# Keys and values of a graph layer set anew: five norm batches, ScalarE shares the row norm, edge preparation moved forward

## The chip, the cores and the metric

One NeuronCore of a Trainium2 chip runs the whole program. The metric is the device time of one execution in microseconds (us); lower is better. The engines are TensorE (PE in the rows), VectorE (DVE), ScalarE (ACT), GpSimd (POOL) and SyncE (SP), which issues most DMAs.

## The reference, cut to what matters

A graph transformer layer on 3125 nodes of 256 channels and 50,000 edges, all in float32:

```
xn   = layernorm(x)
gate = sigmoid(silu(edge @ W1 + b1) @ W2 + b2)          # per edge
aggr = segment_sum(gate * xn[src], dst)
gnn  = xn + silu(concat(xn, aggr) @ U1 + c1) @ U2 + c2
q, k, v = xn @ wq.T, xn @ wk.T, xn @ wv.T               # 4 heads of 64
k, v = layernorm(k), layernorm(v)                       # per head
mix  = (q @ (k.T @ v / S)) @ wo.T + bo                  # per head, no softmax
x    = x + gnn + mix
x    = x + moe(layernorm(x))                            # 16 experts, top 2
```

The change lies in what comes before the edges: `xn`, the keys and values, their norms, and the sum `k.T @ v` over all nodes.

## The kernel before, in words

The 3125 rows lie in 25 tiles of 128 (`NT`). There is no scheduler: each engine runs its own list, written out by hand, and semaphores tie the lists together. The program has four long stretches: the keys and values (to about 100 us of the span), the edges in 98 groups of 512, the node update, and the experts. Only the first is touched.

In it a tile goes this way. VectorE takes mean and variance (`stats`, L1053, and `moments`, L1057). `layer_stats` makes 1/sqrt(variance) for a batch of tiles at once by twelve tiny instructions, each of which waits for the one before (L1048, L1037, L1038, and three rounds of L1040 to L1042); I call them links. Before, there are three batches: tiles 0 to 3, 4 to 9 and 10 to 24. `make_xn` (L1064) then writes the normalised row into one of four buffers; SyncE stores it to DRAM for the gathers of the edges. TensorE transposes it (L1618), ScalarE copies the transpose out (`copy_xt`, L752), and TensorE multiplies it by `wkv` (`project`, L1625, which holds both key and value weights). The head means are taken out of `wkv` itself, once: VectorE sums the heads (L1134), GpSimd subtracts the mean (`centre_wkv`, L573 and L574). ScalarE then copies the product (`drain_kv`, L757) and squares it (L759), and VectorE sums the squares per head (`sum_sq`, L1070).

The head norms need 1/sqrt too, in five batches (`KVCUT`: tiles 0 to 5, 6 to 11, 12 to 17, 18 to 21, 22 to 24), again by twelve links (`kv_seed`, L1083 to L1085, and three times `kv_step`, L1091 to L1093). With them VectorE scales the keys (`scale_k`, L1101) and GpSimd the values (`scale_v`, L566), and TensorE adds the tile to the running sum (`sum_kv`, L1634 and L1635). The sum of tile t comes nine tiles behind the projection (`KLAG = 9`): TensorE's list is "transpose tile t+2, project tile t, sum tile t-9".

Around this stand other duties: GpSimd works out the tables of the edges (`edge_tables`, `edges_left`) and adds the node biases to `x` (`add_biases`, L560), one tile behind each `scale_v`; ScalarE clears the aggregate (`clear`, L767) where keys and values are used up; and the first edge group is prepared behind the last sums (`weights_low` L1145 and L1146, `rbf_low` L1110, TensorE's `up` L1651, ScalarE's silu L795 and cast L798, `h1_low` L1115). The edges begin with `gates(0, 0)` (L1697). GpSimd issues four gathers for each group (L624); `message` (L1251) uses them.

## Time and profile before

| what | value |
|---|---|
| median of 3 runs | 1095.02 us (1093.89 to 1095.49) |
| profiled execution, its own time | 1096.34 us |
| its span | 1094.3 us |
| busy in the span | PE 1042.7, DVE 886.6, POOL 750.1, ACT 689.2 us |
| mean granted TensorE clock | 0.988 of full |

The difference between span and time, 2.0 us, lies outside what the profile covers. Busy shares are a mean over four stretches with different limits: in the first 100 us TensorE waits often, behind that hardly ever. So the table says little on this change, and the rows of the first 130 us say nearly all.

### The profile page before, as it was taken

How to read it: one execution, taken by the hardware profiler on the slowest of the kernel's cores; microseconds unless marked ns; L12 is line 12 of the kernel's file. 1: busy time of each engine (PE TensorE's matmuls, PEld its weight loads, DVE VectorE, ACT ScalarE, POOL GpSimd, SP SyncE). 2: the span in 40 equal slices, each digit the busy share in tenths (PEclk: the TensorE clock that was granted, in tenths of full speed). 3: DMA queues.
4: the chain of work that ended last, by engine and by line, in shares of the span. 5: the costliest groups of instructions: out<-in, count | busy, mean ns of one | idle time of the engine just before them, and what ended most of it. 6: DMA issues, size and time to landing. Idle time of an engine off the chain costs nothing.

```text
span 1094.3 us, 23706 instructions
## 1 busy us (share of the span) xinstructions
PE 1042.7 (95%) x7960; PEld 984.1 (90%) x7960; DVE 886.6 (81%) x1482; ACT 689.2 (63%) x1075; POOL 750.1 (69%) x704
## 2 busy tenths in 40 slices
PE   4897899999999999999999998999899999999995
PEld 2465899999999999999999998998699999999995
DVE  7877888899999988889988883578777777777773
ACT  2563666766666666666666653666277777777763
POOL 5447777777777777777777765550257777777765
PEclk9999999999999999999999999999899999999998
DMA  7211444444455444444455430226178989889961
GB/s 245 77 59 33 141 135 143 141 142 144 141 144 144 142 142 143 137 141 143 142 143 145 142 96 5 75 69 209 27 218 226 234 221 237 215 235 226 233 186 15
DMA packets 118529, 159.75 MB, mean 146 GB/s; under 512 B 20569, under 2 KB 91053, under 8 KB 118445
## 3 DMA queue, kind: packets, MB, share of 16 engines
q0 software_dynamic: 31104, 66.28, 26.2%
q1 hardware_dynamic: 86780, 91.60, 25.9%
q8 instruction: 48, 0.79, 0.3%
q10 hardware_dynamic: 560, 0.79, 0.2%
q14 instruction: 37, 0.30, 0.1%
HBM read 142.42 MB, written 18.17 MB: 147 GB/s over the span
## 4 chain that ended last, share of the span: by engine, by line
PE 87%; DVE 7%; issue 2%; ACT 1%; DMA 1%; DVEq 0%; POOL 0%; POOLq 0%; SPq 0%; ACTq 0%
PE ps L1697 25%; PE ps L1708 16%; PE ps L1906 16%; PE ps L1651 8%; PE ps L1918 8%; PE ps L1752 4%; PE ps L1625 2%; PE ps L1764 2%; PE ps L1777 2%; PE ps L1886 1%; PE ps L1791 1%; DVE st L1053 1%; PE ps L1634 1%; PE ps L1635 1%; PE ps L1832 1%
## 5 line engine op out<-in xcount | busy, mean ns | idle before, releaser
L1697 PE MATMUL ps<-fr 128*128 128x256 f32 x2352 | 305.5, 286 | 3.2 <-DVE fr L1115 3.2
L1697 PEld LDWEIGHTS ps<-fr 128*128 128x128 f32 x2352 | 288.0, 191 | 4.1 <-DVE fr L1115 4.0
L624 POOL DMA_INDIRECT big<-xn_rows,srcs x200 | 219.9, 1100 | 61.3 <-issue 61.3
L624 POOL DMA_INDIRECT hgx<-xn_rows,srcs x192 | 209.6, 1092 | 58.5 <-issue 58.5
L795 ACT ACTIVATE h1f<-ps,b 128x512 f32<-128x512 f32 x196 | 124.1, 684 | 166.4 <-PE ps L1651 165.7
L1708 PEld LDWEIGHTS ps<-oh,big 128*128 128x128 f32 x1568 | 191.3, 193 | 8.6 <-DVE big L1251 0.5
L1906 PE MATMUL ps<-fr 128*128 128x256 f32 x1536 | 190.4, 283 | 1.6 <-issue 1.3
L1708 PE MATMUL ps<-oh,big 128*128 128x96 f32 x1568 | 189.8, 275 | 0.4 <-DVE big L1260 0.4
L1906 PEld LDWEIGHTS ps<-fr 128*128 128x128 f32 x1536 | 186.8, 192 | 2.4 <-issue 2.2
L1115 DVE TENSOR_TENSOR fr<-h1f,fr 128x1024 fp32r<-128x1024 f32 x98 | 120.1, 1225 | 51.7 <-ACT fr L798 51.6
L701 POOL DMA_INDIRECT out<-xnT,idx x60 | 112.9, 1882 | 40.9 <-issue 35.6
L1538 DVE TENSOR_TENSOR fr<-big,fr 128x1024 fp32r<-128x1024 f32 x96 | 117.5, 1224 | 18.1 <-ACT fr L947 17.8
L947 ACT CAST fr<-big 128x1024 fp32r<-128x1024 f32 x95 | 99.7, 1049 | 36.8 <-PE ps L1918 35.8
L1237 DVE TENSOR_TENSOR big<-ps,b2bc 128x1024 f32<-128x1024 f32 x98 | 119.5, 1219 | 1.4 <-PE ps L1697 1.0
L1651 PE MATMUL ps<-fr 128*128 128x512 f32 x392 | 107.7, 396 | 1.9 <-DVE fr L1110 1.9
L802 ACT ACTIVATE big<-big 128x1024 f32<-128x1024 f32 x98 | 103.7, 1058 | 8.9 <-DVE big L1237 8.9
L798 ACT CAST fr<-h1f 128x1024 fp32r<-128x1024 f32 x98 | 102.6, 1047 | 8.5
L1918 PE MATMUL ps<-fr 128*128 128x256 f32 x768 | 99.6, 286 | 0.4 <-DVE fr L1560 0.4
L1918 PEld LDWEIGHTS ps<-fr 128*128 128x128 f32 x768 | 94.0, 192 | 0.7 <-DVE fr L1560 0.7
L687 POOL DMA_INDIRECT hgx<-xn_rows,idx x56 | 59.7, 1067 | 32.0 <-POOL idx L683 22.9
L1651 PEld LDWEIGHTS ps<-fr 128*128 128x128 f32 x392 | 67.6, 190 | 11.0 <-DVE fr L1110 2.1
L1110 DVE TENSOR_TENSOR fr<-rbf,fr 64x512 fp32r<-64x512 f32 x98 | 68.2, 697 | 3.1 <-DVE big L1212 0.2
(241 smaller groups left out, 1413.6 us busy)
## 6 DMA issues: line engine op xcount, KB each, us to landing
big<-in_w SPq DMA_DIRECT2D x128, 256.0 KB, 4.2
rbf<-in_rbf SPq DMA_DIRECT2D x98, 256.0 KB, 2.9
big<-in_w SPq DMA_DIRECT2D x32, 512.0 KB, 4.3
xn_rows<-xn SPq DMA_DIRECT2D x26, 128.0 KB, 2.4
big<-xn_rows,srcs POOLq DMA_INDIRECT x200, 3.2
xn_rows<-hgx SPq DMA_DIRECT2D x24, 128.0 KB, 2.4
hgx<-xn_rows,srcs POOLq DMA_INDIRECT x192, 3.2
out<-x_nodes SPq DMA_DIRECT2D x6, 512.0 KB
```

The costliest lines, as they stand in the source:

```text
L624: pool.indirect_dma_start(hg[i % HB][:, s, :], None, xn_d[:, :], bass.IndirectOffsetOnAxis(srcs[:, col:col + 1], 0))\
L701: pool.indirect_dma_start(out_d[:, :], bass.IndirectOffsetOnAxis(idx[p][:, 2 + s:3 + s], 0), ys[p][:, s, :], None, bounds_check=N - 1, oob ...
L795: act.activation(h1f[:, m, :], ps[:, m, :], ACT.Silu, bias=b1[:, m:m + 1]).then_inc(s_silu, 1)
L802: act.activation(th[p], th[p], ACT.Tanh, scale=0.5).then_inc(s_th, 1)
L1115: dve.tensor_tensor(h1s[p][1], h1f[:, :, :], h1s[p][0].bitcast(f32), ALU.subtract).then_inc(s_hlo, 1)
L1237: dve.tensor_tensor(th[p].rearrange("p (b s) d -> p b (s d)", b=2), ps[:, 2 + 4 * p:4 + 4 * p, :], b2bc[:, :, :].rearrange("p s d -> p (s ...
L1538: dve.tensor_tensor(halves[1], wst[r][p], halves[0].bitcast(f32), ALU.subtract).then_inc(s_wlo[r], 1)
L1651: last = mm(ps[:, m, :], W1s[k][:, m * P:(m + 1) * P], rbs[p], start=k == 0, stop=k == 1)
L1697: last = mm(ps[:, 2 + 4 * p + s // 2, (s % 2) * D:(s % 2 + 1) * D], h1s[p][a][:, c, s * P:(s + 1) * P], W2s[b][:, c, :], start=c == 0 and ...
L1708: last = mm(ps[:, 4 + p, c * w_n:(c + 1) * w_n], msg[p][:, s, c * P:(c + 1) * P], oh[p][:, s, 0:w_n], start=s == 0, stop=s == ET - 1)
L1906: last = mm(ps[:, 2 * m + q, k * SB:(k + 1) * SB], ws[q][a][:, 2 * m + c, k * P:(k + 1) * P], xTs[p][b][:, c, :], start=(c, a, b) == parts ...
L1918: last = mm(ps[:, 4 + p + (2 * s if halves else 0), s * D:(s + 1) * D], hids[p][a][:, k, s * P:(s + 1) * P], ws[r][b][:, k, :], start=k == ...
```

## The change

It does the following, all in the first stretch.

- **Norms of the rows.** Five batches instead of three (`LNCUT`: tiles 0 and 1, 2 to 5, 6 to 11, 12 to 17, 18 to 24). The head sums of `wkv` come behind the first two normalised tiles. `norms` also writes -mean/std, so that ScalarE can make the rows: tiles 2 to 17 are made by `norm_xn` on ScalarE (an activation Identity with scale and bias), the others by VectorE as before. `ROWSAT` and `NORMAT` say at which step of VectorE's loop statistics and batches stand.
- **wkv** is centred in two halves, each with its own signal.
- **Scaling.** `scale_k` stands at the head of a step, ahead of `sum_sq`. The squares have four buffers instead of two. `kv_seed` stands one step of `kv_step` closer to its next ones, the last steps of a batch two together, and behind step 24 the last nine `scale_k` are threaded with the preparation of the first edge group.
- **Biases.** `add_biases` runs two tiles at a step from GpSimd's step 3 on and is over at step 15; GpSimd reads the flag there too. The three last instructions of `edges_left` stand between two `scale_v`.
- **Edge preparation.** The high halves of W1 and W2 are cast at ScalarE's steps 13 and 14, the low halves made at VectorE's steps 16 and 17, ahead of the last sums; `clear` starts five steps later. TensorE's `up(0, 0, 0)` stands behind the sum of tile 18 instead of 22, and TensorE reads the flag behind it.
- **Products without use.** 14 products `ones x ones` into an unused bank ahead of the first transpose, 6 ahead of the first projection, 6 behind it.

```diff
+KVAT = (7, 13, 19, 23, NT)
+LNCUT = (0, 2, 6, 12, 18, NT)
+ROWSAT = {0: (6, 12), 2: (12, 14), 3: (14, 16), 4: (16, 18), 9: (18, 20), 10: (20, 22), 11: (22, NT)}
+NORMAT = {0: 2, 5: 3, 12: 4}
+ACTXN = (LNCUT[1], LNCUT[4])
+SQB = 4
+CLEARAT = 15
+BIASAT = {t: (2 * t - 6, min(2 * t - 4, NT)) for t in range(3, 16)}
...
             for t in range(NT):
                 scale_v(t)
-                add_biases(t)
+                if t == 1:
+                    edges_marked()
+                for u in range(*BIASAT.get(t, (0, 0))):
+                    add_biases(u)
+                if t == 15:
+                    pool.wait_ge(s_flag, 1)
+                    left = pool.value_load(flag[0:1, 0:1], min_val=0, max_val=E)
...
+            def norm_xn(t):
+                if not ACTXN[0] <= t < ACTXN[1]:
+                    return
+                act.wait_ge(s_ln, sum(t >= a for a in LNCUT))
+                if t >= XB:
+                    act.wait_ge(s_xnst[t % XB], t // XB * 16)
+                    act.wait_ge(s_tp, t - XB + 3)
+                act.activation(xn[t % XB], x[:, t, :], ACT.Identity, scale=rstd[:, t:t + 1], bias=nmx[:, t:t + 1])\
+                    .then_inc(s_xn, 1)
             copy_xt(0)
             copy_xt(1)
+            norm_xn(2)
             for t in range(NT):
+                norm_xn(t + 3)
                 if t + 2 < NT:
                     copy_xt(t + 2)
                 drain_kv(t)
-                if t > KLAG:
-                    clear(t - KLAG - 1)
+                if t >= CLEARAT:
+                    clear(t - CLEARAT)
...
+            def norms(k):
+                q = slice(LNCUT[k], LNCUT[k + 1])
+                layer_stats(LNCUT[k], LNCUT[k + 1] - LNCUT[k])
+                dve.scalar_tensor_tensor(nmx[:, q], mv[:, q, 0], -1.0, rstd[:, q], ALU.mult, ALU.mult)\
+                    .then_inc(s_ln, 1)
...
+            for t in range(NT):
+                if ACTXN[1] <= t + 3 < NT:
+                    dve.wait_ge(s_xn, t + 3)
                     make_xn(t + 3, XB, s_xn, s_xnst, s_tp)
-                if t >= KLAG:
+                if KLAG <= t < NT:
                     scale_k(t - KLAG, (t - KLAG) % 2)
+                if 2 <= t < NT:
+                    sum_sq(t - 2)
+                if t in ROWSAT:
+                    rows(*ROWSAT[t])
+                if t in KVAT[:-1]:
+                    kv_seed(KVAT.index(t))
+                    kv_step(KVAT.index(t), 0)
+                if t - 1 in KVAT[:-1]:
+                    kv_step(KVAT.index(t - 1), 1)
+                    kv_step(KVAT.index(t - 1), 2)
+                if t in NORMAT:
+                    norms(NORMAT[t])
...
+            for u in range(NT - KLAG, NT):
+                scale_k(u, u % 2)
+                if u - (NT - KLAG) < 2:
+                    sum_sq(u + KLAG - 2)
+                if u == NT - 7:
                     rbf_low(0, 0, 0)
+                    kv_seed(last)
+                    kv_step(last, 0)
+                if u == NT - 6:
+                    kv_step(last, 1)
+                    kv_step(last, 2)
+                if u == NT - 4:
                     rbf_low(0, 1, 1)
...
+            def warm(n):
+                for _ in range(n):
+                    mm(ps[:, 7, 0:P], ones[:, :], ones[:, :], start=True, stop=True)
+            warm(14)
             transpose_xn(0, 0, 0, s_tp, s_xn)
             transpose_xn(1, 1, 0, s_tp, s_xn)
-            pe.wait_ge(s_cen, 1)
+            warm(6)
...
-                if t == NT - 3:
-                    pe.wait_ge(s_wlow, 1)
+                if t == NT - 7:
+                    pe.wait_ge(s_wlow, 2)
                     up(0, 0, 0)
+                    pe.wait_ge(s_flag, 1)
+                    left = pe.value_load(flag[0:1, 0:1], min_val=0, max_val=E)
```

What stands where, at the three places on which the argument rests. First the head of VectorE's list (`st` and `mv` are statistics, `rstd` the links' result, `v_p` the head sums of `wkv`), before:

```order
L1053 BN_STATS st<-x_nodes 128x6 x4
L1134 TENSOR_REDUCE v_p<-wkv 128x16
L1057 BN_AGGR mv<-st 128x2 x4
L1048 TENSOR_SCALAR v_c<-mv 128x4
L1037 TENSOR_SCALAR v_a<-v_c 128x4
...
L1064 TENSOR_SCALAR xn<-x_nodes,mv,rstd 128x256 x2
L1064 TENSOR_SCALAR hgx<-x_nodes,mv,rstd 128x256 x2
L1053 BN_STATS st<-x_nodes 128x6 x6
```

and in the change:

```order
L1090 BN_STATS st<-x_nodes 128x6 x2
L1094 BN_AGGR mv<-st 128x2 x2
L1079 TENSOR_SCALAR v_c<-mv 128x2
L1068 TENSOR_SCALAR v_a<-v_c 128x2
...
L1085 SCALAR_TENSOR_TENSOR hgx<-mv,rstd 128x2
L1101 TENSOR_SCALAR xn<-x_nodes,mv,rstd 128x256 x2
L1178 TENSOR_REDUCE v_p<-wkv 128x16
L1090 BN_STATS st<-x_nodes 128x6 x4
```

The first rows no longer wait for four tiles and for the sum of `wkv`, which moved behind them; a norm batch of four follows at once.

Second, GpSimd behind its tables of edges (`oh<-big,kvr` is `scale_v`, `x_nodes<-x_nodes,cb` is `add_biases`), before:

```order
L600 TENSOR_TENSOR rbf<-rbf 128x392
L566 TENSOR_TENSOR oh<-big,kvr 128x256
L560 TENSOR_TENSOR x_nodes<-x_nodes,cb 128x256
L566 TENSOR_TENSOR oh<-big,kvr 128x256
L560 TENSOR_TENSOR x_nodes<-x_nodes,cb 128x256
```

and in the change:

```order
L576 TENSOR_TENSOR oh<-big,kvr 128x256 x2
L612 TENSOR_SCALAR rbf<-dstf 128x392
L613 TENSOR_SCALAR rbf<-dstf 128x392
L614 TENSOR_TENSOR rbf<-rbf 128x392
L576 TENSOR_TENSOR oh<-big,kvr 128x256 x2
L570 TENSOR_TENSOR x_nodes<-x_nodes,cb 128x256 x2
L576 TENSOR_TENSOR oh<-big,kvr 128x256
L570 TENSOR_TENSOR x_nodes<-x_nodes,cb 128x256 x2
```

From the fourth value tile on three instructions stand in a step instead of two, and the last nine steps hold only the `scale_v`.

Third, the end of VectorE's list before the edges (`oh<-big,kvr` here is `scale_k`, `fr<-W` is `weights_low`, `fr<-rbf` is `rbf_low`, `hgx` and `kvr` are the links of a head batch), before:

```order
L1093 SCALAR_TENSOR_TENSOR kvr<-hgx,kvr 128x24
L1101 TENSOR_TENSOR oh<-big,kvr 128x2x128
L1145 TENSOR_TENSOR fr<-W,fr 128x256
L1146 TENSOR_TENSOR fr<-W,fr 128x512
L1101 TENSOR_TENSOR oh<-big,kvr 128x2x128 x2
L1110 TENSOR_TENSOR fr<-rbf,fr 64x512 x2
L1101 TENSOR_TENSOR oh<-big,kvr 128x2x128 x3
L1115 TENSOR_TENSOR fr<-h1f,fr 128x1024
```

and in the change:

```order
L1138 TENSOR_TENSOR oh<-big,kvr 128x2x128
L1147 TENSOR_TENSOR fr<-rbf,fr 64x512
L1120 TENSOR_SCALAR hgx<-ssq 128x24
...
L1130 SCALAR_TENSOR_TENSOR kvr<-hgx,kvr 128x24
L1138 TENSOR_TENSOR oh<-big,kvr 128x2x128 x2
L1147 TENSOR_TENSOR fr<-rbf,fr 64x512
L1138 TENSOR_TENSOR oh<-big,kvr 128x2x128 x3
L1152 TENSOR_TENSOR fr<-h1f,fr 128x1024
```

The low halves of the weights are gone from the end, and the first `rbf_low` stands ahead of the last head batch instead of behind it.

## Rows read from the trace of the kernel before

**Rows 1.** The page: the chain's shares of the span, by engine.

```profile
PE 87%; DVE 7%; issue 2%; ACT 1%; DMA 1%; DVEq 0%; POOL 0%; POOLq 0%; SPq 0%; ACTq 0%
```

**Rows 2.** Chain that ended last, in order of time: start, us, what.

```profile
14.09 0.73 DVE xn L1064 x2
...
43.73 0.71 PE ps L1634 x4
...
125.38 3.36 PE ps L1708 x16
...
134.35 2.90 PE ps L1697 x24
...
648.32 2.90 PE ps L1697 x24
```

**Rows 3.** Timeline of PE: start, us, engine, line, operation, [idle before <-releaser].

```profile
15.70 3.78 PE L1625 MATMUL ps<-wkv,xnT 128*128 128x512 f32 x4
...
46.65 0.61 PE L1634 MATMUL ps<-oh 128*128 128x129 f32 x4
...
47.74 1.88 PE L1625 MATMUL ps<-wkv,xnT 128*128 128x512 f32 x4
...
85.80 0.61 PE L1634 MATMUL ps<-oh 128*128 128x129 f32 x4
...
106.22 3.13 PE L1697 MATMUL ps<-fr 128*128 128x256 f32 x24 [2.69 <-DVE fr L1115]
```

**Rows 4.** Timeline of DVE, same columns.

```profile
5.17 0.75 DVE L1053 BATCH_NORM_STATS2 st<-x_nodes 128x6 f32<-128x256 f32 x2 [5.17 <-DMA x_nodes<-in_x]
...
21.57 0.74 DVE L1053 BATCH_NORM_STATS2 st<-x_nodes 128x6 f32<-128x256 f32 x2
...
22.63 0.41 DVE L1064 TENSOR_SCALAR xn<-x_nodes,mv,rstd 128x256 f32<-128x256 f32 x1
22.96 0.68 DVE L1070 TENSOR_REDUCE ssq<-h1f 128x8 f32<-128x512 f32 x1
...
34.43 0.17 DVE L1048 TENSOR_SCALAR v_c<-mv 128x15 f32<-128x15 f32 x1
...
36.95 0.41 DVE L1064 TENSOR_SCALAR hgx<-x_nodes,mv,rstd 128x256 f32<-128x256 f32 x1
```

**Rows 5.** Timelines of POOL and DVE where both are busy.

```profile
9.68 1.90 POOL L574 TENSOR_TENSOR wkv<-wkv,v_p 128x1024 f32<-128x1024 f32 x1
...
20.27 1.20 POOL L587 TENSOR_SCALAR rbf<-rel 128x392 f32<-128x392 f32 x1
...
20.84 0.17 DVE L1041 SCALAR_TENSOR_TENSOR v_b<-v_a,v_c 128x6 f32<-128x6 f32 x1
...
87.56 0.72 POOL L560 TENSOR_TENSOR x_nodes<-x_nodes,cb 128x256 f32<-128x256 f32 x1
...
88.36 0.54 DVE L1084 TENSOR_SCALAR hgx<-hgx 128x24 int32<-128x24 int32 x1
```

**Rows 6.** Timeline of ACT in a step with a sum.

```profile
50.15 0.60 ACT L759 ACTIVATE h1f<-ps 128x512 f32<-128x512 f32 x1
50.63 0.62 ACT L767 COPY big<-before 128x512 f32<-128x512 f32 x1
```

**Rows 7.** Windows: stretch, length, busy of PE, PEld, DVE, ACT, POOL, granted clock, DMA share, GB/s.

```profile
126.00:128.00 2.00, 2.00 (x11) 2.00 (x11) 2.00 (x2) 1.73 (x3) 1.50 (x2) 0.50 0.48 157
```

**Rows 8.** Gathers and first message: timelines, the page's groups and its DMA issues.

```profile
103.63 1.24 POOL L624 DMA_INDIRECT big<-xn_rows,srcs  x1 [0.68 <-issue]
...
119.46 1.21 DVE L1251 SCALAR_TENSOR_TENSOR big<-big 128x1024 f32<-128x1024 f32 x1
...
L624 POOL DMA_INDIRECT big<-xn_rows,srcs x200 | 219.9, 1100 | 61.3 <-issue 61.3
L624 POOL DMA_INDIRECT hgx<-xn_rows,srcs x192 | 209.6, 1092 | 58.5 <-issue 58.5
...
big<-xn_rows,srcs POOLq DMA_INDIRECT x200, 3.2
```

More of the change, by code:

```diff
@@ L216, in gps_layer @@
         idx = [sb(f"idx{i}", [P, ET], i32) for i in range(2)]
-        sq = [h1f[:, i, :] for i in range(2)]
+        sq = [h1f[:, i, :] for i in range(2)] + [part(hgx, 1024 * i, 512) for i in range(2)]
+        nmx = part(hgx, 1760, NT)
         oflat = [oh[i][:, :, :].rearrange("p s w -> p (s w)") for i in range(2)]
@@ L573, in centre_wkv @@
                 link(pool.tensor_scalar(v_p[:, :], v_p[:, :], 1.0 / HD, None, ALU.mult))
-                pool.tensor_tensor(heads, heads, v_p[:, :].unsqueeze(2).to_broadcast([P, DC * 8, HD]), ALU.subtract)\
-                    .then_inc(s_cen, 1)
+                for c in range(DC):
+                    h = slice(c * 8, c * 8 + 8)
+                    pool.tensor_tensor(heads[:, h, :], heads[:, h, :],
+                                       v_p[:, h].unsqueeze(2).to_broadcast([P, 8, HD]), ALU.subtract).then_inc(s_cen, 1)
             def edge_tables():
@@ L775, in _ @@
                 drain_kv(t)
-                if t > KLAG:
-                    clear(t - KLAG - 1)
-            act.wait_ge(s_par, 16 * NPAR)
-            for dst, src in ((W1s[0], W1[:, :]), (W2s[0], W2[:, :, :])):
-                act.copy(dst, src).then_inc(s_whi, 1)
+                if t >= CLEARAT:
+                    clear(t - CLEARAT)
+                if t == 13:
+                    act.wait_ge(s_par, 16 * NPAR)
+                    act.copy(W1s[0], W1[:, :]).then_inc(s_whi, 1)
+                if t == 14:
+                    act.copy(W2s[0], W2[:, :, :]).then_inc(s_whi, 1)
+            for u in range(NT - CLEARAT, NT - KLAG):
+                clear(u)
             act.sem_inc(s_silu, 4)
-            act.wait_ge(s_sq, NT + 2)
+            act.wait_ge(s_sq, NT + SQB)
             def edges(n0, h0):
@@ L1129, in get_x @@
                 return stats(t)
-            for t in range(4):
+            for t in range(LNCUT[1]):
                 last = get_x(t)
+            link(last)
+            for t in range(LNCUT[1]):
+                last = moments(t)
+            link(last)
+            norms(0)
+            for t in range(LNCUT[1]):
+                make_xn(t, XB, s_xn, s_xnst, s_tp)
             dve.wait_ge(s_wkv, 16)
@@ L1135, in _, with weights_low @@
                 .then_inc(s_wsum, 1)
-            link(last)
-            for t in range(4):
-                last = moments(t)
-            link(last)
-            layer_stats(0, 4)
-            for t in range(3):
-                make_xn(t, XB, s_xn, s_xnst, s_tp)
-            def weights_low():
-                dve.wait_ge(s_whi, 2)
-                dve.tensor_tensor(W1s[1], W1[:, :], W1s[0].bitcast(f32), ALU.subtract)
-                dve.tensor_tensor(W2s[1], W2[:, :, :], W2s[0].bitcast(f32), ALU.subtract).then_inc(s_wlow, 1)
+            def weights_low(k):
+                dve.wait_ge(s_whi, k + 1)
+                halves, of = ((W1s, W1[:, :]), (W2s, W2[:, :, :]))[k]
+                dve.tensor_tensor(halves[1], of, halves[0].bitcast(f32), ALU.subtract).then_inc(s_wlow, 1)
             def rows(a, b):
```

44 lines of the change are left out of this document (15 added, 29 removed).

## The prediction

> **What bounds the kernel now.** I read the page first: TensorE is busy for 1042.7 of 1094.3 us and carries 87% of the chain that ended last [rows 1]. That is a mean. The chain in order of time says where it does not hold. Up to 43.73 us nearly every link of it is VectorE; from there to 84.3 us it is TensorE without a gap; then VectorE and ScalarE hand work to each other until the first gate product at 106.22; and from about 125 us on it is TensorE alone, one edge group each 5.59 us: (648.32 - 134.35) / 92 [rows 2, 3]. The change touches nothing behind 106.22, so I take it as a shift: what the first gate product gains, the kernel gains, if the gathers keep up.
>
> I cut the first 106 us in three: to the first sum of keys and values (S0, 43.73), from S0 to S15 (85.80), from S15 to the gates (106.22) [rows 2, 3]. The reader is to see who is late in each.
>
> **Part one, to S0.** VectorE starts at 5.17, when the first rows of x are there, makes the first row at 14.09, and is busy from then on without rest [rows 2, 4]. Prices: statistics and moments of two tiles 1.06 (21.57 to 22.63), so 0.43 a tile in larger lots, where one chain of waits serves more; a norm batch 2.52 (34.43 to 36.95), that is 0.21 a link; a sum of squares 0.60; a row 0.41 [rows 4].
> Now: 5.17 + 1.06 + 2.5 gives the first row at 8.8 instead of 14.09. Two rows and the head sums of wkv (1.1, the same instruction as before) end at 10.6. Batch of tiles 2 to 5: 1.7 + 2.5 + 0.2 for the added instruction; GpSimd centres wkv under it (1.90, then 0.7 for cb), and two links wait for that as one link takes 0.54 under GpSimd's 0.72 [rows 5]: about 1.2. It ends at 16.2. Batch of 6 to 11: 2.6 + 2.7 + 0.6 of the same waits, 22.1. Three pairs of tiles 3.2, seven sums of squares 4.2, batch of 12 to 17 2.7, the twelve links of the first head batch 2.8 (wider, 0.235 each): 35.0. The first scale_k 0.8, so S0 at 35.8 instead of 43.73: 7.9 earlier.
> Is TensorE ready by then? A tile takes 2.80 in part two, and its sum 0.88 of that (47.74 - 46.65, less 0.2 for a transpose [rows 3]); so a projection with its transpose takes 1.94 here, and T2, the transpose of tile 2, needs row 2, made by ScalarE at 16.5, so the projections 1 to 9 run from 17.0 to 34.5. Yes, by 1.3. ScalarE's step holds two instructions of 512 columns, 0.49 from start to start [rows 6], and two of 256, for which I take 0.35 each: 1.7 of 1.94. The Identity on SBUF data has no row; its bounds are 0.27 and 0.62 (the clear [rows 6]), and even the upper leaves 1.95, so it costs nothing; it may cost 0.1 a step for eight steps.
> The 26 products: the first projection takes 3.78 where a later one takes 1.88 [rows 3], so it ran at the lower of the two clock levels (1.2 GHz), the later ones at 2.4. With products from 4.7 us on the first projection should run at the upper level. It is worth nothing here, since VectorE sets S0; and it costs at most 1.3 (six products of 0.215) where TensorE waits for row 2 anyway.
>
> **Part two, S0 to S15.** TensorE's pace is 2.80 a tile: (85.80 - 43.73) / 15 [rows 2, 3]. Nothing waits, so here nothing can be won, only lost. VectorE gives up the rows 12 to 17 (six of about 0.5) but brings along seven tiles of statistics (3.0), the last norm batch (2.7), and the low weight halves (2.0). A scale_k may start when the sum two before it is done, and is needed 4.7 later; that is the slack. In steps 9 to 11 VectorE does 2.4 of work in 2.8 and enters step 12 at about 41.8. There the norm batch meets GpSimd, which now runs a scale_v and two biases, 2.2 of 2.8: while GpSimd is in a two-input instruction, VectorE gets one link through (0.54 for one of 0.18 [rows 5]). Six of thirteen links are hit, 0.4 each: 2.4. So scale_k(4) ends at 48.6 and was due at 46.9: 1.7 lost. Once more at S6, behind the second head batch: 0.7. Later head batches lag within the slack: GpSimd itself stands still until the links are done, which frees them. S15 falls at 35.8 + 42.1 + 2.4 = 80.3, 5.5 earlier than 85.80.
>
> **Part three, S15 to the gates.** Before: 20.4. The last batches of head links, the low weights (2.0), and two rbf_low run between the sums, TensorE idles, and h1_low comes last, the gates wait 2.69 for it [rows 3]. Now: S16 waits 1.2 for the links of tiles 18 to 21; nine sums at 0.88 are 7.9; behind S18 ScalarE still has three clears, its flag and the cast of the edge inputs, rbf_low 0.75, up(0) and the last head links, together 2.7 more than the sums hide; the second half of the links 1.3; handovers 0.9. That is 14.0, so the gates start at 94.3. Silu and cast of group 0 (about 4 with their table load) lie under S19 to S24. Part three gains 6.4.
>
> **Gathers.** They start when GpSimd has done its last value tile: 103.63 before [rows 8], about 93.6 now, since the biases no longer lie between. That is 10.0 earlier where the gates are 11.9 earlier. A group is four gathers of 1.10 + 0.30 and lands 3.2 later [rows 8]: first group there 8.8 after the start, at 102.4. The first message stood 13.2 behind the gates (119.46), so it comes at 107.5. The 1.9 is hidden with 5 to spare.
>
> **Sum.** 7.9 - 2.4 + 6.4 = 11.9. The profiled execution took 1096.34, 1.3 above the median; its 1094.3 of span go to 1082.4, the execution to 1084.4. On the median: 1095.02 - 11.9, rounded 1083.0.
>
> **A rule weighed.** There are two cases in [rows 5]: a link under GpSimd's two-input instruction takes 0.54 instead of 0.18, one under its TENSOR_SCALAR takes 0.17, as if alone. The Trainium skill (SBUF — State Buffer, section "SBUF: two separate sides") says of the port pair that VectorE and GpSimd share: it is "an exclusive lock, not a bandwidth split", held for a whole instruction. By that every GpSimd instruction holds a link; the trace agrees for the two-input ones only. What it would make here is a rival below.
>
> **The rivals.**
> *Every GpSimd instruction holds the links (4%).* The tables of edges run from 17.6 to about 32 and are twelve instructions, one link through in each. Of the 38 links that I place there, 26 come later, 0.21 to 0.235 each: S0 at 41.6 instead of 35.8, gain 6, 1089. Against it stands the 0.17 [rows 5]. The rule named above belongs here.
> *VectorE becomes the bound in part two (15%).* For it: GpSimd's share there goes from 1.35 to 2.2 of 2.8, and scale_k, at 0.42 alone, is hit too. If each head batch costs what step 12 does, three times 2.4, the gain is 7: 1088.
> *No stall at all (17%).* If GpSimd and VectorE fall out of step, 2.4 and 1.2 are won, and the gain is 15.5: 1079.5. For it: before the change part two has no gap at all, though GpSimd and VectorE meet there too.
> *The gathers set the pace (5%, the slower one).* All 392 gathers take 429.5 + 119.8 = 549.3, 5.605 a group, against TensorE's 5.59 [rows 2], and GpSimd waits for nothing but issue [rows 8]. They run freely in the gaps that VectorE leaves. With another phase to VectorE they may take more; from 1.40 to 1.431 each eats the whole gain (11.9 / 392), to 1.47 gives 98 x 0.28 = 27 us: 1098 to 1110. Against it: they take that time because they are held at just TensorE's period, and messages never wait for them.
> *The change wins only the start (4%).* If the chain in part three is really the cast of the edge inputs and it comes no sooner, 6.4 shrinks to 2: 1087.5.
>
> **How the numbers follow.** The likeliest case, as worked out, has 55%, with a range of its own of 1081 to 1085.5: one clock fall more or less. At 125.38 sixteen products ran at granted clock 0.50 and took 3.36 [rows 2, 7], 1.7 more than at full clock, after a wait of TensorE; it may come again or not. The range goes from the no-stall case to the VectorE case: 1079.0 to 1088.5. It leaves out the slower rival, part of the first one and the ends of others, 2 in 10. A measurement of this kernel can tell 0.2% (2.2 us) from no change. Faster: all but the gathers rival and some unforeseen loss, 0.93; within 0.2% 0.03; slower 0.04.
>
> **What would show it.** First projection at 12 and at 1.9 us, not 3.8; first sum at 35 to 36.5; between S0 and S15 gaps of PE in front of sums 4 and 6, released by VectorE's scale_k; ScalarE under 1.7 a step; gates at 93 to 96; first gather about 1 before it; edge groups still 5.59 apart. Wrong would make me: PE waiting for rows of ScalarE in steps 1 to 9, DVE waiting for x at tile 4, links of 1 us under TENSOR_SCALAR, or messages that wait for gathers.

## The result and the profile after

The changed kernel takes 1086.67 us (median of 4 runs, 1086.27 to 1087.07) against 1095.24 before (4 runs, 1093.89 to 1095.49): ratio 0.9924, 95% interval 0.9907 to 0.9941, 8.6 us faster. Forecast were 1083.0, range 1079.0 to 1088.5; the likeliest case had a range of its own, 1081 to 1085.5, and the result lies outside that one. The profiled execution took 1086.27, its span 1084.3; the span before was 1094.3, so 10.0 went there. The rest of the difference is in which execution was profiled: 1.10 above its median before, 0.40 below it now, and 10.07 - 1.50 = 8.57. One thing on the runs below: e1 to e4 ran on another chip, on which every kernel, the one before too, took 1165 to 1198 us, with TensorE idle for 32 to 39 us between 140 and 640 us for nothing that the profile shows and a granted clock of 0.94 to 0.96 there, and e4's trace is of one of the slower executions.

The page after, the chain's shares beside [rows 1] and the gathers beside [rows 8]:

```profile
PE 86%; DVE 8%; issue 2%; ACT 1%; DMA 1%; POOL 0%; DVEq 0%; POOLq 0%; ACTq 0%; PEldq 0%
...
L644 POOL DMA_INDIRECT big<-xn_rows,srcs x200 | 218.7, 1093 | 61.2 <-issue 61.2
L644 POOL DMA_INDIRECT hgx<-xn_rows,srcs x192 | 210.2, 1095 | 58.5 <-issue 58.5
...
big<-xn_rows,srcs POOLq DMA_INDIRECT x200, 3.2
```

The timeline of PE after, beside [rows 3] (columns as there):

```profile
5.14 5.47 PE L1689 MATMUL ps<-ones 128*128 128x128 f32 x28 [5.14 <-POOLq L561]
...
12.22 1.89 PE L1675 MATMUL ps<-wkv,xnT 128*128 128x512 f32 x4
...
16.51 0.93 PE L1666 MATMUL ps<-ident,hgx 128*128 128x128 f32 x4 [1.06 <-ACT hgx L795]
...
35.88 0.71 PE L1684 MATMUL ps<-oh 128*128 128x129 f32 x4 [0.99 <-DVE oh L1138]
...
48.82 0.71 PE L1684 MATMUL ps<-oh 128*128 128x129 f32 x4 [1.41 <-DVE oh L1138]
...
55.65 0.71 PE L1684 MATMUL ps<-oh 128*128 128x129 f32 x4 [0.93 <-DVE oh L1138]
...
81.07 0.61 PE L1684 MATMUL ps<-oh 128*128 128x129 f32 x4
...
82.33 0.71 PE L1684 MATMUL ps<-oh 128*128 128x129 f32 x4 [0.22 <-DVE oh L1138]
...
86.09 1.16 PE L1705 MATMUL ps<-fr 128*128 128x512 f32 x4 [0.38 <-issue]
88.10 0.71 PE L1684 MATMUL ps<-oh 128*128 128x129 f32 x4 [0.84 <-DVE oh L1138]
...
90.34 0.71 PE L1684 MATMUL ps<-oh 128*128 128x129 f32 x4 [1.10 <-DVE oh L1138]
...
96.32 3.11 PE L1754 MATMUL ps<-fr 128*128 128x256 f32 x24 [0.30 <-PE ps L1685]
...
114.98 3.20 PE L1765 MATMUL ps<-oh,big 128*128 128x96 f32 x16
```

S0 stands at 35.88 (43.73 before), S15 at 81.07 (85.80), the first gate product at 96.32 (106.22): 7.85 us are won up to S0, 3.12 of them are lost again up to S15, and 5.17 are won behind it, 9.90 in all. TensorE waits for a scale_k of VectorE in front of S4 (1.41) and S6 (0.93), and in part three for S19 (0.84) and S20 (1.10).

ScalarE in step 3 after, and VectorE and GpSimd in step 12, same columns:

```profile
18.52 0.60 ACT L795 ACTIVATE xn<-x_nodes,hgx,rstd 128x256 f32<-128x256 f32 x1 [0.17 <-issue]
19.02 0.35 ACT L770 COPY xnT<-ps 128x256 f32<-128x256 f32 x1
19.28 0.58 ACT L775 COPY big<-ps 128x512 f32<-128x512 f32 x1
19.75 0.60 ACT L777 ACTIVATE h1f<-ps 128x512 f32<-128x512 f32 x1
...
43.48 0.66 DVE L1079 TENSOR_SCALAR v_c<-mv 128x7 f32<-128x7 f32 x1
44.18 0.65 DVE L1068 TENSOR_SCALAR v_a<-v_c 128x7 int32<-128x7 int32 x1
44.86 0.17 DVE L1069 TENSOR_SCALAR rstd<-v_a 128x7 int32<-128x7 int32 x1
...
46.97 0.65 DVE L1073 SCALAR_TENSOR_TENSOR rstd<-v_b,rstd 128x7 f32<-128x7 f32 x1
...
48.26 0.17 DVE L1085 SCALAR_TENSOR_TENSOR hgx<-mv,rstd 128x7 f32<-128x7 f32 x1
...
43.40 1.40 POOL L570 TENSOR_TENSOR x_nodes<-x_nodes,cb 128x256 f32<-128x256 f32 x2
...
46.19 1.40 POOL L570 TENSOR_TENSOR x_nodes<-x_nodes,cb 128x256 f32<-128x256 f32 x2
```

The Identity of 256 columns takes 0.60 (0.49 to the next start); ScalarE's step nearly fills the 1.94 of a projection, and behind row 2 (16.51, waited for 1.06) TensorE never waits for it up to S0. The last norm batch, thirteen links, has five of 0.59 to 0.66 where one alone takes 0.17. Four of them lie under GpSimd's pairs of bias adds (43.40 to 44.80, 46.19 to 47.59) and one, 0.59 at 45.67, under a `scale_v`. Each of the five ends 0.02 to 0.03 behind the end of the GpSimd instruction that it lies under, so VectorE gets one link through for each instruction.

### The profile page after: what moved, and what is told of

Its sections match the earlier page's. It is cut to its first block, busy times and chain, and to the rows that moved or that the text cites. A ratio compares the mean times of both kernels' runs of the same rounds, so it can differ in the third digit from the quotient of the medians.

```text
span 1084.3 us, 23845 instructions
## 1 busy us (share of the span) xinstructions
PE 1047.0 (97%) x8012; PEld 989.6 (91%) x8012; DVE 886.2 (82%) x1495; ACT 696.5 (64%) x1091; POOL 749.8 (69%) x705
## 4 chain that ended last, share of the span: by engine, by line
PE 86%; DVE 8%; issue 2%; ACT 1%; DMA 1%; POOL 0%; DVEq 0%; POOLq 0%; ACTq 0%; PEldq 0%
PE ps L1754 25%; PE ps L1961 16%; PE ps L1765 16%; PE ps L1705 8%; PE ps L1973 8%; PE ps L1807 4%; PE ps L1819 2%; PE ps L1832 2%; PE ps L1675 1%; PE ps L1941 1%; DVE st L1090 1%; PE ps L1846 1%; DVE ssq L1107 1%; PE ps L1887 1%; PE ps L1684 1%
## 5 line engine op out<-in xcount | busy, mean ns | idle before, releaser
L978 ACT CAST fr<-big 128x1024 fp32r<-128x1024 f32 x95 | 99.7, 1049 | 36.9 <-PE ps L1973 35.8
```

## The experiments

Twelve kernels ran. Landmarks of the traces carry the verdicts. Each kernel has one trace, but its parts repeat closely where the kernels are alike there (S0 to S15 is 45.17 to 45.21 in the changed kernel, e1, e7 and e10), while the executions of one kernel differ by 1 to 6 us. The landmarks are S0, S15 and the gates as in [rows 3], then the last sum of the edge part and the end of the span. Cells are empty where the other chip or e5's other output leaves nothing to compare.

| kernel | S0 | S0 to S15 | S15 to gates | first gather | gates to last sum | behind it | median |
|---|---|---|---|---|---|---|---|
| before | 43.73 | 42.07 | 20.42 | 103.63 | 553.75 | 434.3 | 1095.24 |
| changed | 35.88 | 45.19 | 15.25 | 95.33 | 553.39 | 434.6 | 1086.67 |
| e1 | 36.49 | 45.17 | 16.40 | 97.06 | | | |
| e2 | 42.30 | 46.39 | 15.26 | 102.95 | | | |
| e3 | 36.37 | 44.94 | 17.82 | 95.14 | | | |
| e4 | 36.33 | 44.31 | 18.61 | 98.57 | | | |
| e5 | 36.32 | 42.69 | 14.94 | 92.95 | 553.45 | | |
| e6 | 36.51 | 43.49 | 17.79 | 96.79 | 553.46 | 435.9 | 1089.54 |
| e7 | 36.12 | 45.18 | 15.24 | 95.55 | 553.45 | 436.2 | 1087.74 |
| e8 | 36.38 | 43.50 | 17.68 | 96.57 | 553.44 | 434.6 | 1087.46 |
| e9 | 36.39 | 43.08 | 15.19 | 93.66 | 553.76 | 434.4 | 1086.34 |
| e10 | 36.21 | 45.21 | 14.82 | 95.25 | 553.48 | 437.5 | 1089.05 |
| e11 | 36.29 | 43.07 | 14.58 | 92.86 | 553.43 | 434.3 | 1083.88 |
| e12 | 36.01 | 47.62 | 14.94 | 97.57 | 553.48 | 439.4 | 1091.72 |

S0 falls at 36.0 to 36.5 in all kernels that left part one alone, against 35.88; in e1, e3 and e4 the norm batches of tiles 6 to 11 and 12 to 17 end 0.2 to 0.6 later than in the changed kernel, with other links of them under GpSimd's instructions. So the parts are compared by their own lengths. The ratios to before of e1 to e4 are 0.9986 (0.9949 to 1.0023), 1.0038 (0.9989 to 1.0088), 0.9944 (0.9903 to 0.9985) and 0.9985 (0.9940 to 1.0030): too wide to rank them, and the changed kernel itself did not run on that chip. So these four times say nothing on the times that were expected, and the traces are read up to the gates.

**e1: without the 26 products.** The three calls are gone:

```diff
-            warm(14)
...
-            warm(6)
...
-                    warm(6)
```

> The changed kernel without its 26 products of ones by ones; nothing of the output hangs on them. My theory: they buy nothing, because VectorE sets S0. The first projection takes about 3.8 us again instead of 1.89, it ends near 16.0, before row 2 is transposed at 16.5, S0 stays at 35.9 and the median at 1086.7 (within 0.5). Rival: TensorE is still at the lower clock when T2 and the second projection come (16.5), these take 1 to 2 us longer, the 0.99 us that S0 waits for scale_k is used up, S0 falls at 36.5 to 37 and the median at 1087.3 to 1088.

The first projection took 3.75 again (at 12.11), and S0 still waited 1.55 for scale_k (0.99 in the changed kernel):

```profile
12.11 3.75 PE L1675 MATMUL ps<-wkv,xnT 128*128 128x512 f32 x4 [1.92 <-POOL wkv L586]
...
36.49 0.71 PE L1684 MATMUL ps<-oh 128*128 128x129 f32 x4 [1.55 <-DVE oh L1138]
```

The products buy nothing up to S15, as forecast. S0 at 36.49 touches what the rival named, but not by its way: the wait for scale_k grew instead of being used up, and e3 to e9, which keep the products, have S0 at 36.1 to 36.5 too. The 1.15 more in part three are two sums at the lower clock (1.03 and 1.07 in place of 0.71 and 0.61). In the changed kernel the last of the products ends 75 us ahead of these sums; that they have nothing to do with it is my reading, and no second trace shows it.

**e2: all rows by VectorE.**

```diff
-ACTXN = (LNCUT[1], LNCUT[4])
+ACTXN = (2, 2)
...
+            make_xn(2, XB, s_xn, s_xnst, s_tp)
```

> The changed kernel with all rows made by VectorE again (tiles 2 to 17 as well), everything else as changed. My theory: VectorE sets part one, so nine or ten rows of 0.33 to 0.41 us more before S0 put it at 39.3 to 39.8 instead of 35.88; in part two six more rows meet GpSimd's two biases and the stalls in front of S4 and S6 grow from 2.3 to 3 or 4 us. Median 1090.5 to 1092. Rival: ScalarE's step of four instructions (1.94 us) holds TensorE in the steps 1 to 9, and VectorE had room; then S0 stays within 1 us of 35.9 and the median within 1 us of 1086.7.

S0 came at 42.30, 6.4 later: more than either theory, whose ten rows cost 3.9 at most. TensorE's timeline shows where:

```profile
16.11 0.89 PE L1667 MATMUL ps<-ident,hgx 128*128 128x128 f32 x4 [0.74 <-DVE hgx L1101]
...
23.90 0.69 PE L1667 MATMUL ps<-ident,xn 128*128 128x128 f32 x2 [5.18 <-DVE xn L1101]
```

VectorE works in order. Row 4 now stands behind the statistics and the links of tiles 6 to 11, and TensorE is idle for 5.18 until it comes; projection 2 then runs at the lower clock (3.62 for 1.88) and projection 3 in part (2.34), which costs 2.2, and projections 3 to 9 last until 42.2, with S0 right behind them. So ScalarE's rows are worth 6.4 in this order: projection 2 starts 4.9 later (24.38 for 19.45) because of the place of the row in VectorE's queue, the lower clock adds 2.2, and the 0.99 that TensorE had to spare is used up. Behind S0 the stalls did not grow to 3 or 4 as I had expected: S4 waits 1.97, S6 not at all, and S0 to S15 is 1.2 longer, in part at the lower clock.

**e3: the head of the edge part at its old place.** Casts of the weights behind the last drain, their low halves behind scale_k(19), rbf_low behind scale_k(21), up(0) behind S22:

```diff
...
-                if t == NT - 7:
+                if t == NT - 3:
                     pe.wait_ge(s_wlow, 2)
                     up(0, 0, 0)
```

> The changed kernel with the head of the edge part at its old place: weights cast behind the last drain, low halves behind scale_k(19), rbf_low behind scale_k(21), up(0) behind S22, and the clears from step 10 on. My theory: part three (S15 to the gates, 15.25 us as changed, 20.4 before) goes back to 19 to 20.5, because h1_low comes last again and the gates wait for it; S15 stays at 81 or comes up to 0.8 earlier, since VectorE is free of the two low halves in steps 16 and 17. Median 1090.5 to 1092. Rival: part three was won by the head links of the last tiles coming earlier, not by the edge head; then the gates move by less than 1.5 us and the median stays under 1088.2.

```profile
99.13 5.49 PE L1751 MATMUL ps<-fr 128*128 128x256 f32 x24 [2.87 <-DVE fr L1148]
```

The gates wait 2.87 for h1_low again [rows 3], and part three grows by 2.57 to 17.82, half of the 5.17 that the change wins there; I had expected 19 to 20.5, the rival less than 1.5 more. The other half must lie in what e3 keeps, the order of links and keys in the last batches, but no run takes that back alone. After the wait the 24 gate products ran at the lower clock, 5.49 for 3.11, so behind the gates it costs 2.4 more.

**e4: one bias add a step. e6: the pairs two steps later. e5: adds with one input.** e5 adds the constant 1.0 and so leaves out the node biases; that changes the work behind the node part (its 1104 us aren't comparable, TensorE has 8164 matmuls instead of 8012).

```diff
-BIASAT = {t: (2 * t - 6, min(2 * t - 4, NT)) for t in range(3, 16)}
+BIASAT = {t: (t, t + 1) for t in range(NT)}                              # e4
+BIASAT = {t: (2 * t - 10, min(2 * t - 8, NT)) for t in range(5, 18)}     # e6
...
-                pool.tensor_tensor(x[:, t, :], x[:, t, :], cb[:, 0, :], ALU.add)
+                pool.tensor_scalar(x[:, t, :], x[:, t, :], 1.0, None, ALU.add)  # e5
```

> The changed kernel with one add of the biases behind each scale_v, as before the change, instead of two from step 3 to 15. My theory: GpSimd's two-input instructions under the last norm batch make the stalls in front of S4 (1.41) and S6 (0.93); with half the adds there S4 loses at most 0.7 and S6 nothing, S15 comes 1.3 to 2 us earlier; but from S15 on one add stands behind each scale_v, and GpSimd ends its last one later: the gathers start 1 to 2 us behind the gates instead of 1.0 ahead of them. The gates come 1 to 2 earlier, and the messages have 4 or more to spare, so the median is 1085 to 1086. Rival: the stall is VectorE's own load (norm batch of thirteen links beside scale_k and a sum of squares); then S4 and S6 stay as they are, and the gates come later by what scale_v waits in part three, 0.5 to 1.5 us: 1087.2 to 1088.2.

> The changed kernel with the pairs of bias adds from step 5 to 17 instead of 3 to 15, so that GpSimd has none while VectorE makes the last norm batch in step 12. My theory: the batch runs at 0.2 a link, the stall in front of S4 falls from 1.41 to under 0.5; S6 (0.93) stays or falls by 0.3; S15 comes 1.0 to 1.7 us earlier after S0, but two more pairs stand behind scale_v(16) and (17) and may delay a value by up to 0.7 there. Gates 0.5 to 1.5 us earlier after S0, time 0.5 to 1.5 below the changed kernel's. Rival: what step 12 loses is VectorE's own load, and the adds only move into the third head batch (step 19 to 20) with the same loss: nothing is won, within 0.5.

> The changed kernel, in which each add of the node biases (GpSimd, two inputs, 0.7 us) is an add of the constant 1.0 (GpSimd TENSOR_SCALAR, one input, about as long: 1.20 us for 392 columns is 0.8 for 256). The node biases are left out, so the output isn't the reference's. My theory: only two-input instructions of GpSimd hold VectorE's links, so the last norm batch (thirteen links in step 12) takes 2.6 to 3.2 us instead of 4.9, the stall in front of S4 falls from 1.41 to under 0.5, and the gates come 1 to 2.3 us earlier after S0. Rival: GpSimd holds the links whatever it runs, as a lock on the port pair for a whole instruction says; then the batch stays at 4.5 us or more and the stalls stay, or grow since 0.8 is longer than 0.7.

The norm batch of step 12, first link to end, took 4.95 in the changed kernel, 3.75 in e5. Links in e5, VectorE and GpSimd:

```profile
44.38 0.42 DVE L1069 TENSOR_SCALAR rstd<-v_a 128x7 int32<-128x7 int32 x1
44.83 0.32 DVE L1071 TENSOR_TENSOR v_a<-rstd 128x7 f32<-128x7 f32 x1
45.18 0.17 DVE L1072 SCALAR_TENSOR_TENSOR v_b<-v_a,v_c 128x7 f32<-128x7 f32 x1
...
43.92 1.66 POOL L570 TENSOR_SCALAR x_nodes<-x_nodes 128x256 f32<-128x256 f32 x2
```

A link that meets a one-input instruction takes 0.32 to 0.42, a two-input one 0.65, alone 0.17. So neither theory holds as stated: the one-input kind costs too, about 0.2 where the other costs 0.48, and only for a part of its length, since the link at 45.18 takes 0.17 although the instruction of 44.74 to 45.58 still runs. With the milder kind the stalls are gone: S4 and S6 don't wait, S0 to S15 falls by 2.50 and all to the gates by 2.8. That is the 2.4 of my sum.

e4 wins less and by another way than I had expected. S4 waits 0.33, S6 0.81, and S0 to S15 is 0.88 shorter; but the norm batch takes 5.16 there, since each scale_v and each single add beside it still holds a link. It only starts 0.7 earlier behind S0; that VectorE met fewer adds before it is likely, but not shown apart. The price comes from S15 on: TensorE waits for GpSimd's scale_v (0.27 to 1.38, five times) and 2.14 for S19, and part three is 3.4 longer, partly at the lower clock. e6 cures S4 (the batch takes 3.09) and pays in step 19 and 20, where the links of tiles 18 to 21 are held, as its rival said; S16 waits

```profile
83.24 1.13 PE L1684 MATMUL ps<-oh 128*128 128x129 f32 x4 [2.20 <-DVE oh L1138]
```

and sums at the lower clock. S0 to the gates is 0.84 longer, where I had expected 0.5 to 1.5 less: the wrong sign. Its time, 1089.54, is 2.9 above the changed kernel's, as its span is: 0.6 of that lies ahead of S0, 0.8 up to the gates and 1.4 behind the edge part (see the clock below).

**e7, e8: the last six clears behind the first silu.** e8 has e6's line too.

```diff
-            for u in range(NT - CLEARAT, NT - KLAG):
-                clear(u)
...
                 silu(0, 0)
+                if type(n0) is int:
+                    for u in range(NT - CLEARAT, NT - KLAG):
+                        clear(u)
```

> The changed kernel with ScalarE's last six clears behind the first silu and its cast (ScalarE stands idle there for 10 us), instead of ahead of the casts of the edge inputs. My theory: in part three the cast of the edge inputs stands behind these clears (82.24 to 84.3); 2 us earlier, VectorE makes rbf_low right behind scale_k(18), at 84.4 instead of 85.30, and up(0), the last head batch, S19 and S20 come 0.8 to 0.9 earlier: the gates come 0.5 to 1.0 us earlier after S15, and the time is that much below the changed kernel's. Rival: scale_k(18) and the links set the pace there, or VectorE pays back in h1_low; then the gates stay within 0.3 us.

> Both edits together: pairs of bias adds two steps later, and the last six clears behind the first silu. If both theories hold, the gains add: gates 1.0 to 2.5 us earlier after S0 than in the changed kernel (60.4), the time 1.0 to 2.5 us below it. If the adds behind scale_v(16) and (17) hold VectorE in part three, the second gain is eaten: no more than the better one alone.

ScalarE's timeline in e7:

```profile
82.47 0.62 ACT L785 COPY big<-before 128x512 f32<-128x512 f32 x1
84.87 1.14 ACT L818 CAST fr<-rbf 128x512 fp32r<-128x512 f32 x2 [1.78 <-DVE ssq L1108]
```

Nothing is won (15.24 for 15.25): with the clears gone the cast of the edge inputs stands still for 1.78. VectorE's last sum of squares ends at 84.02; from there to the cast ScalarE reads the flag of the edge part into a register, 0.8, which the kernel does behind that wait (in the changed kernel the same read takes from 83.8 to 84.65). The clears had only hidden both. e8 is e6 again: its expectation of 1.0 to 2.5 less to the gates, or the better of the two alone, came out as 0.74 more.

**e9, e10, e11: what these results point to.** e9 puts the adds where VectorE makes no links, and the last five behind the last gather. e10 lets the casts go ahead of the wait that e7 showed (the silu alone writes where the squares lie), with e7's clears; the read of the flag comes earlier with them. e11 is both.

```diff
+BIASAT = {2: (0, 2), 7: (2, 5), 8: (5, 8), 9: (8, 11), 10: (11, 14), 12: (14, 17), 13: (17, 20)}
...
             edges(0)
+            for u in range(20, NT):
+                add_biases(u)
...
-            act.wait_ge(s_sq, NT + SQB)
...
                 rbf_high(1, 0, 1)
+                if type(n0) is int:
+                    act.wait_ge(s_sq, NT + SQB)
                 silu(0, 0)
```

> The changed kernel with the node biases placed by what VectorE does beside them: two behind scale_v(2), three each behind scale_v(7) to (10), three each behind (12) and (13), and the last five behind the last gather, where GpSimd stands idle for 5.4 us in the changed kernel (its last gather ends at 643.27, its next work starts at 648.63). None lies under the last norm batch or under a batch of head links. My theory, from the run in which the adds had one input (S0 to gates 57.6 us instead of 60.4): the waits in front of S4, S6, S12 and S16 go, S0 to gates takes 57.5 to 58.2, the time falls by 2.2 to 2.9 below the changed kernel's. Rival: three adds a step (0.61 + 3 x 0.73 = 2.8) leave GpSimd no slack against TensorE's 2.8; scale_v comes late, TensorE waits for POOL in front of S8 to S14, 0.2 a step or more, and half of the gain goes: 58.8 to 59.6.

> The changed kernel with ScalarE's wait for the last sum of squares behind the two casts of the edge inputs (only the silu writes where the squares lie), and the last six clears behind the first silu. The run with the clears alone moved showed what the cast waits for: VectorE's last sum of squares, 1.78 us, and not the clears. My theory: now the cast starts at 82.7 to 83.2 instead of 84.65, rbf_low right behind scale_k(18) at 84.5, up(0), S19 and S20 come 0.7 to 0.8 earlier, and so do the gates: S15 to gates 14.5 instead of 15.25, the time 0.5 to 0.8 below the changed kernel's. Rival: the two casts (1.14) and scale_k(18) end together anyway, or GpSimd and VectorE meet otherwise in S21 to S24: within 0.3.

> The planned biases and the cast ahead of the wait together. If they add, S0 to gates takes 56.8 to 57.5 us (60.4 in the changed kernel), and the time is 2.8 to 3.6 below the changed kernel's, 11.5 to 13 below the one before. The fall of the clock behind the gates may come or not, which is 1.7 either way. Rival: with S16 earlier, the cast's flag or the edge inputs' arrival sets up(0), and the second gain is lost: 57.6 to 58.2.

PE in e11:

```profile
53.98 0.71 PE L1688 MATMUL ps<-oh 128*128 128x129 f32 x4 [0.53 <-DVE oh L1142]
...
85.64 0.71 PE L1688 MATMUL ps<-oh 128*128 128x129 f32 x4 [1.03 <-DVE oh L1142]
...
87.88 0.71 PE L1688 MATMUL ps<-oh 128*128 128x129 f32 x4 [1.10 <-DVE oh L1142]
...
93.94 3.11 PE L1758 MATMUL ps<-fr 128*128 128x256 f32 x24 [0.38 <-PE ps L1689]
...
112.51 1.92 PE L1769 MATMUL ps<-oh,big 128*128 128x96 f32 x16
```

S0 to the gates takes 58.27 in e9 (57.5 to 58.2 was expected; S6 still waits 0.52) and 57.65 in e11 (56.8 to 57.5 was expected), against 60.44. Both gains are there in e11, 2.17 and 0.62, so they add, though 57.65 lies in the range of the rival in which the second one is lost. On the medians e9 missed: 1086.34 is 0.33 below the changed kernel's, where 2.2 to 2.9 was expected; its profiled execution, 1084.84, is the fastest of its five. In e10 the cast starts at 83.09 and up(0) comes 0.73 earlier behind S15, as expected, but only 0.43 of it reaches the gates, since VectorE's last head links, not the cast, then hold S19 and S20. e11 takes 1083.88 us (1083.33 to 1086.85; ratio to before 0.9903, 0.9889 to 0.9918), 2.8 below the changed kernel (2.8 to 3.6 was expected) and the best kernel here: its interval still overlaps the changed kernel's, but the gates stand 2.38 and the last sum 2.34 earlier. e10's median is 2.4 above the changed kernel's, where 0.5 to 0.8 below it was expected, though S15 to the gates is shorter; in its trace the excess lies behind the last sum (437.5 for 434.6), see below.

**e12: keys scaled last.** Sum of squares and head links ahead of scale_k, statistics behind it, as before the change.

```diff
-                if KLAG <= t < NT:
-                    scale_k(t - KLAG, (t - KLAG) % 2)
                 if 2 <= t < NT:
                     sum_sq(t - 2)
...
+                if KLAG <= t < NT:
+                    scale_k(t - KLAG, (t - KLAG) % 2)
                 if t in ROWSAT:
```

> The changed kernel with VectorE's order inside a step as before the change: the sum of squares and the head links ahead of scale_k, the rows of statistics behind it. My theory: in a step with links the key stands behind 1.5 to 4 us more, so the waits of TensorE in front of S4 to S6 (behind the links of step 13 and 14), S10 to S11 and S14 to S16 grow, 0.6 to 1.5 each: S0 to S15 takes 46.5 to 48.5 us instead of 45.19, and the time is 1.5 to 3.5 above the changed kernel's. Rival: a scale_k has 4.7 us of slack in either order, as in the kernel before, where this part had no gap: within 0.5 of the changed kernel.

```profile
50.86 1.23 PE L1684 MATMUL ps<-oh 128*128 128x129 f32 x4 [3.32 <-DVE oh L1138]
```

S4 alone waits, 3.32, because scale_k(4) now stands behind the norm batch, a sum of squares and half of the head links; no other wait of part two grows, S6 has none, where I had named S5, S6 and S10 to S16 as well. S0 to S15 is 2.43 longer, S0 to the gates 2.12. The time, 1091.72, is 5.0 above the changed kernel's, more than the 1.5 to 3.5 expected; in the trace, of its slowest execution (1093.35), 4.8 of excess lie behind the last sum, which the edit doesn't touch. The ratio to before is 0.9963 (0.9950 to 0.9976). So the new order is worth 2.4 up to S15 in the changed kernel. In the kernel before, with the old order and no norm batch in part two, no sum waited there.

## Why the prediction was right, and where it was off

The result is in the range, and the three parts came as described, with sizes that were off. That the range held is in part its width: its upper end came from the rival in which VectorE becomes the bound, and that rival's mechanism did not occur.

*Part one, 7.9 forecast, 7.85 measured.* S0 at 35.8 against 35.88; first row 8.57 (8.8), batches done at 15.8, 21.8 and 30.1, links at 34.7 (35.0); the first projection 1.89 instead of 3.78; S0 released by VectorE with TensorE 0.99 early (1.3 forecast). e1 shows that the 26 products are worth nothing up to S15. What I had priced too low is ScalarE's Identity: 0.60, 0.49 from start to start, where I took 0.35. It cost nothing, as the working said of its upper bound. e2 adds what the sum did not hold: these rows are worth 6.4. No run puts the old norm batches back, so what they won rests on the timeline alone (first row 8.57 for 14.09).

*Part two, gain 5.5 forecast, 4.73 measured.* Places and releasers were right (S4 1.41 for 1.7, S6 0.93 for 0.7, both released by scale_k), and e5 and e9 show the cause: with adds of one input, or with the adds elsewhere, the same order of VectorE takes 42.7 to 43.1. The 2.4 for held links is right only because two errors cancel: I had six links at 0.4 each, there are five at 0.42 to 0.49. The term was 0.7 short: S0 to S15 took 45.19, not 44.5. 42.1 of bare pace and 2.34 of these two waits make 44.4; the rest is handovers behind waits, the small product of the flag, and a late S12. The rival that VectorE becomes the bound in this part is refuted by the same rows: behind S6 no sum waits up to S15.

*Part three, 14.0 forecast, 15.25 measured; the step that failed in size.* "nine sums at 0.88 are 7.9" is one sum too few: S0, S15 and the gates are all taken at their starts, so S15 itself belongs here, and ten sums are 8.8, 0.9 more. "S16 waits 1.2" was 0.22. The handovers and small waits, 0.9 in the sum, came to 2.1. "Behind S18 ... 2.7 more than the sums hide" was the place and the size (S18 to S19 takes 3.53, 2.65 more than a sum), and so was the 1.3 for the second half of the links (S19 to S20, 1.36 more than a sum). But it is not the clears that hold the cast of the edge inputs, as I had it; it is the last sum of squares and the read of the flag behind it (e7), and S19 and S20 wait for links that stand behind rbf_low on VectorE (e10, e11: an earlier rbf_low brings them forward by 0.43). S22 and S24 wait 0.27 each for scale_v, h1_low is held by GpSimd (1.64 for 1.23) and ends at 95.85, 0.2 ahead of the end of S24. Of the 6.4 that I gave this part 5.17 came; e3 assigns 2.57 of it to the edge head; the other 2.6 were not tested apart.

*Gathers: right in the verdict, wrong in the margin.* They began 8.3 earlier (95.33; 10.0 was forecast), message 0 at 109.22, and nothing waited there. But "5 to spare" holds for the first message only. At the other end, DVE's last message and the gather that ends last, in the changed kernel, e7 and e11:

```profile
648.07 1.23 DVE L1299 SCALAR_TENSOR_TENSOR big<-big 128x1024 f32<-128x1024 f32 x1
...
642.32 0.95 POOL L644 DMA_INDIRECT big<-xn_rows,srcs  x1 [0.30 <-issue]
```

```profile
648.35 1.23 DVE L1300 SCALAR_TENSOR_TENSOR big<-big 128x1024 f32<-128x1024 f32 x1 [1.77 <-DMA big<-xn_rows,srcs]
...
644.42 0.94 POOL L644 DMA_INDIRECT big<-xn_rows,srcs  x1 [0.30 <-issue]
...
649.99 3.70 PE L1766 MATMUL ps<-oh,big 128*128 128x96 f32 x16 [2.03 <-DVE big L1309]
```

```profile
645.38 1.58 DVE L1303 SCALAR_TENSOR_TENSOR big<-big 128x1024 f32<-128x1024 f32 x1 [1.46 <-DMA big<-xn_rows,srcs]
...
641.74 0.95 POOL L644 DMA_INDIRECT big<-xn_rows,srcs  x1 [0.30 <-issue]
```

In e7 the last message comes 3.0 behind the end of the last gather and waits 1.77 for it; in the changed kernel 4.8 behind it, so it had 1.8 to spare. All 392 gathers took 547.9 from first to last in the changed kernel and e9, and 549.8 in e5 to e8 and e10 to e12. Of the 1.9 more, 1.1 arise between the 21st and the 29th gather (124 to 136 us), where single ones take 1.82 instead of 1.34 at most; the pace is then the same up to the end, where the last but one takes 1.93 in e7 and 1.30 in the changed kernel. The changed kernel and e9 are also the two of these whose clock falls at 113 to 115 us (below), just ahead of that; before the change, with a fall at 125 us, it is 548.7. The gathers start 1.0 to 1.1 ahead of the gates in these kernels, so the start does not part them. The groups of GpSimd's gathers from 95 to 200 us, changed kernel and e7 (busy, mean ns, idle before):

```profile
L644 POOL DMA_INDIRECT big<-xn_rows,srcs x40 | 43.9, 1099 | 12.4 <-issue 12.4
```

```profile
L644 POOL DMA_INDIRECT big<-xn_rows,srcs x40 | 45.3, 1132 | 12.4 <-issue 12.4
```

The 1.4 more are of this kind of gather; the other kind (`hgx<-xn_rows,srcs`) takes 0.3 less in e7 there. So gathers and TensorE are a tie at 5.59 a group. The rival "gathers set the pace", which I gave 5%, names a mechanism that is there (another phase to VectorE, longer gathers), at a price of 1.9 us and not the 12 from which it would have decided.

*The clock.* That the clock fall at 125 us may come again or not, for 1.7, is wrong in its price. It recurred in the changed kernel (114.98, sixteen products in 3.20) and in e9, and not in e5 to e8 and e10 to e12; yet gates to last sum is 553.4 to 553.8 with it and without: what TensorE saves there it gives back in front of the last sum, which waits for the last gather's message (0.36 and 0.70 with the fall, 2.03 to 2.09 without). What does move the time lies behind the edge part, which the change doesn't touch. Windows of the changed kernel and of e12 (length, busy of PE, PEld, DVE, ACT, POOL, granted clock, DMA share, GB/s):

```profile
640.00:680.00 40.00, 36.48 (x294) 36.09 (x294) 20.26 (x50) 14.94 (x27) 23.18 (x19) 0.96 0.09 27
...
720.00:800.00 80.00, 73.27 (x521) 66.74 (x520) 64.77 (x216) 42.17 (x105) 21.84 (x21) 0.94 0.42 123
```

```profile
640.00:680.00 40.00, 34.50 (x253) 34.04 (x252) 16.23 (x38) 11.89 (x21) 23.56 (x18) 0.83 0.09 25
...
720.00:800.00 80.00, 73.07 (x509) 66.81 (x509) 63.86 (x227) 40.77 (x105) 20.64 (x18) 0.91 0.38 114
```

The granted clock from 640 to 800 us puts the kernels in order: with 0.96 or 0.97 (before, changed, e8, e9, e11) the rest behind the last sum took 434.3 to 434.6, with 0.95 (e6) 435.9, 0.94 (e7) 436.2, 0.93 (e10) 437.5 and 0.91 (e12) 439.4. That is up to 5 us between kernels whose gates differ by less. It goes with the medians of e6, e7, e10 and e12, which are 1.1 to 5.0 above the changed kernel's, but each has one trace only. In e7, e10 and e12 the last sum itself ran at the lower level (3.70 for 2.00), behind a wait of 2.0; but e6, e8 and e11 had that wait too and kept the clock. What decides is open, and wasn't tried.

*The sum.* 11.9 forecast at the gates, 9.90 measured: 0.05 less in part one, 0.72 in part two, 1.2 in part three. Behind the gates it is 0.36 better, then 0.26 worse, which makes the 10.0 of the span; on the medians 8.57 are left, as said above. The terms that were mis-sized are the handovers of part two (nothing in the sum, 0.7 measured) and, in part three, the tenth sum and the handovers, against which the wait for S16 was priced too high.

*The rule weighed.* By the Trainium skill (SBUF — State Buffer, "SBUF: two separate sides"), a GpSimd instruction that starts first keeps the shared ports for its whole length from a VectorE instruction that needs them, one with two inputs in SBUF or in a mode that uses both ports. For two-input instructions of GpSimd the traces agree: a held link ends 0.02 to 0.05 behind the end of that instruction (44.83 behind 44.80, 47.62 behind 47.59 above). For one-input ones they don't: in e5 a link of two inputs that meets the start of one (44.83, instruction from 44.74 to 45.58) ends 0.41 behind that start, and the next ones take 0.17 while it still runs; only the link of one input at 44.38 was held to the end of the instruction before. [rows 5] show only the second half of this. The link ahead of the one that they show was held too, under the same instruction of 1.20, for 0.2:

```profile
20.44 0.36 DVE L1040 TENSOR_TENSOR v_a<-rstd 128x6 f32<-128x6 f32 x1
```

So "as if alone" was read from one row of two. The measurement decides: both kinds hold a link, the one-input kind mostly for a part of its length. The rival built on the rule (S0 at 41.6) did not come.

## What to carry to other kernels

Place a second engine's filler work by what the first engine does beside it: here the same 25 adds cost 2.2 us more or less up to the edges (e9), depending on whether short dependent links lie under them. When a piece of queued work seems to delay an instruction, look for the wait that it hides before moving it (e7: a sum of squares and a read of a flag); and when a stage is shortened, look at the far end of whatever runs alongside at a fixed pace, since its margin at the start says nothing about the end.
